# Spectral layers of a vision tower: inverse along h for two pairs at once in four banks, turning steps in one pair of banks

## The reference

```python
def spectral_conv(x, w1, w2):
    x_ft = jnp.fft.rfft2(x)
    out_ft = out_ft.at[:, :, :M1, :M2].set(jnp.einsum('bixy,ioxy->boxy', x_ft[:, :, :M1, :M2], w1))
    out_ft = out_ft.at[:, :, -M1:, :M2].set(jnp.einsum('bixy,ioxy->boxy', x_ft[:, :, -M1:, :M2], w2))
    return jnp.fft.irfft2(out_ft, s=(h, w))
...
for i in range(LAYERS):
    x1 = spectral_conv(h, w1, w2)
    x2 = jnp.einsum('bchw,oc->bohw', h, conv_w[i]) + conv_b[i][None, :, None, None]
    h = layer_norm(x1 + x2, ln_g[i], ln_b[i])
    if i < LAYERS - 1:
        h = gelu(h)
```

## Time and profile before

| | us |
|---|---|
| median of 3 runs | 5721.86 |
| lowest, highest | 5716.95, 5734.56 |
| profiled execution, its own time | 5729.41 |
| its span | 5727.7 |
| PE busy | 5285.1 (92%) |
| DVE busy | 4230.7 (74%) |
| ACT busy | 3896.4 (68%) |
| POOL busy | 630.8 (11%) |

### The profile page before, as it was taken

How to read it: one execution, slowest core, us unless ns; L and a number is a source line. 1 busy time by engine, 2 the same in 40 slices (tenths; PEclk the granted TensorE clock), 3 DMA queues, 4 the chain that set the end, 5 groups by cost and what they waited for, 6 DMA issues and landing times.

```text
span 5727.7 us, 135011 instructions
## 1 busy us (share of the span) xinstructions
PE 5285.1 (92%) x43556; PEld 2997.1 (52%) x43556; DVE 4230.7 (74%) x7712; ACT 3896.4 (68%) x6261; POOL 630.8 (11%) x943
## 2 busy tenths in 40 slices
PE   5887789999999999999999999999999999868778
PEld 2444456666666666666666654433333333334443
DVE  5888899999998999999999975555555555454553
ACT  5898776788666788666888656677777777523333
POOL 0133100233000233000233000000000000000000
PEclk9999999999999999999999999999999999877888
DMA  1334467667676667677676762221111111000000
GB/s 65 124 137 148 137 189 215 217 215 230 200 228 206 217 215 230 201 228 221 211 228 224 210 183 70 75 60 51 46 52 52 52 52 52 13 4 4 7 7 4
DMA packets 397185, 756.31 MB, mean 132 GB/s; under 512 B 245041, under 2 KB 303410, under 8 KB 331322
## 3 DMA queue, kind: packets, MB, share of 16 engines
q1 hardware_dynamic: 377402, 704.04, 38.8%
q0 software_dynamic: 19456, 48.01, 3.7%
HBM read 397.49 MB, written 354.42 MB: 131 GB/s over the span
## 4 chain that ended last, share of the span: by engine, by line
PE 81%; DVE 9%; issue 5%; ACT 3%; SPq 1%; DVEq 0%; ACTq 0%; DMA 0%
PE ps_y L914 18%; PE ps_y L907 9%; PE ps_t L926 9%; PE ps_t L1016 8%; PE ps_t L935 8%; PE ps_f L948 4%; PE ps_f L1001 3%; PE ps_s L893 3%; PE ps_f L986 3%; PE ps_s L961 3%; PE ps_t L1025 2%; PE ps_t L346 2%; PE ps_y L883 2%; ACT big L1169 1%; PE ps_f L336 1%
## 5 line engine op out<-in xcount | busy, mean ns | idle before, releaser
L1146 ACT ACTIVATE big<-ps_y 128x512 f32<-128x512 f32 x1280 | 777.0, 607 | 762.2 <-PE ps_y L914 699.6
L914 PEld LDWEIGHTS ps_y<-conv_now,big 128*128 128x128 f32 x8192 | 993.2, 191 | 520.2 <-issue 520.2
L1309 DVE TENSOR_REDUCE big<-big 128x16 f32<-128x512 f32 x1280 | 841.8, 679 | 522.5 <-ACT big L1146 522.3
L914 PE MATMUL ps_y<-conv_now,big 128*128 128x128 f32 x8192 | 1147.2, 283 | 0.0
L1302 DVE TENSOR_TENSOR big<-big 128x512 f32<-128x512 f32 x1280 | 932.1, 748 | 69.3 <-PE ps_t L926 62.2
L1155 ACT ACTIVATE big<-ps_t 128x512 f32<-128x512 f32 x1024 | 622.4, 608 | 334.2 <-PE ps_t L935 328.5
L926 PE MATMUL ps_t<-ident,big 128*128 128x128 f32 x5120 | 790.5, 277 | 43.9 <-DVE big L1302 42.5
L1162 ACT ACTIVATE big<-ps_t,g_now 128x512 f32<-128x512 f32 x1024 | 809.0, 790 | 9.3 <-PE ps_t L926 8.0
L1150 ACT ACTIVATE big<-ps_y 128x512 f32<-128x512 f32 x1280 | 780.1, 609 | 0.0
L926 PEld LDWEIGHTS ps_t<-ident,big 128*128 128x128 f32 x5120 | 587.6, 142 | 260.9 <-issue 204.8
L935 PE MATMUL ps_t<-ident,big 128*128 128x128 f32 x4096 | 654.4, 283 | 55.9 <-ACT big L1155 55.9
(11 more groups left out here) (180 smaller groups left out, 6419.0 us busy)
## 6 DMA issues: line engine op xcount, KB each, us to landing
hstore<-big SPq DMA_DIRECT2D x256, 1024.0 KB, 4.0
big<-hstore SPq DMA_DIRECT2D x256, 1024.0 KB, 5.3
xmodes<-x_out SPq DMA_DIRECT2D x128, 312.0 KB, 4.4
y_kt<-ymodes SPq DMA_DIRECT2D x512, 78.0 KB
ymodes<-y_st SPq DMA_DIRECT2D x192, 144.0 KB, 3.0
mix_room<-xmodes SPq DMA_DIRECT2D x48, 336.0 KB, 7.1
mix_room<-xmodes SPq DMA_DIRECT2D x48, 288.0 KB, 6.2
ymodes<-y_st SPq DMA_DIRECT2D x64, 192.0 KB, 3.4
```

What stands on the lines that cost most here:

```text
L914: last = mm(ps_y[:, wh, 128 * b:128 * b + 128], h_in[k // 2][:, at:at + 128], conv_now[:, :], start=False, stop=(b == 3))
L1146: af(y_sq[wh], ps_y[:, wh, :], ACT.Square).then_inc(s["sq_done"], 1)
L1309: v_.tensor_reduce(ss[:, k // 2, at:at + 16], groups(y_sq[wh]), AX.X, ALU.add).then_inc(s["ss_done"], 1)
```

## The change

Where the front is a layer and the back is not yet the head (`both` in the code), `inv_h` runs in slots 0 and 2 only and does both pairs of its half quad: eight matmuls in eight tiles, the even pair into ps_y and the odd pair into ps_f. `conv`, `square` and `keep_y` of an odd slot use ps_f (`y_of`). The steps with a turn (`inv_w`, `fwd_h`, `fwd_w`) all use ps_s, each with a wait for DVE's turn of the step ahead of it. `fwd_w` moves from the end of slot 1 to the middle of it, behind the first conv. `mix` of these quads goes to ps_y and stands ahead of the first conv of slots 1 and 3. On DVE, `turn_modes` moves from slot 2 to slot 1, behind `normed` and the products' sums, and `mix` behind `normed`. In the head `inv_h` stays with one pair at a time.

In all stages the turns write adjacent elements. To undo that, the matmuls of `inv_h` and `fwd_w` read runs of 16 or 13 adjacent elements and write their result to PSUM with 32 elements between neighbours.

```diff
-            def inv_h(n, k):
+            def inv_h(n, k, both):
...
+                for odd in odds:
+                    for image in range(2):
+                        for wh in range(2):
+                            r, half = slice(64 * image + 32 * wh, 64 * image + 32 * wh + 32), image ^ odd
+                            mm(y_of(odd, both)[64 * half:64 * half + 64, wh, :].rearrange("p (w o) -> p o w", o=32), c_inh[r, :],
+                               z_kx[j][r, :].rearrange("p (o w) -> p o w", w=32)[:, :, 16 * odd:16 * odd + 16],
+                               start=True, stop=False)
...
-                            last = mm(ps_s[at:at + 32, sx, 0:RUN], c_fww[r, :], t_w[r, j, 512 * sx:512 * sx + RUN],
+                            last = mm(ps_s[at:at + 32, sx, 0:RUN].rearrange("p (k c) -> p c k", c=32), c_fww[r, :],
+                                      t_w[r, j, :].rearrange("p (c k) -> p c k", k=32)[:, :, 16 * sx:16 * sx + KX],
...
-                        fwd_h(n - 1, 0, mixed)
+                        fwd_h(n - 1, 0, ps_s if both else ps_f, 0 if both else mixed, 0, n - 1 if both else 0, 0)
...
-                        inv_h(n, k)
-                        conv(k, 0)
+                            wait(pe, "tw_done", 2 * n - 3)
+                        if k % 2 == 0:
+                            wait(pe, "mix_read", mixed)
+                            inv_h(n, k, True)
+                        elif visit is not None:
+                            mix(*visit, ps_y, 2 * (4 * n + k))
+                        conv(k, 0, True)
+                        if k == 1 and back2 in STORED:
+                            fwd_w(n - 2, 2 * i + 2, 0)
...
-                v_.transpose(z_kx[j].rearrange("p (w o) -> p o w", o=32), flat(of).rearrange("p (k o) -> p o k", o=32)
+                v_.transpose(z_kx[j].rearrange("p (o w) -> p o w", w=32), flat(of).rearrange("p (k o) -> p o k", o=32)
...
-                    if k == 2 and back2 in STORED:
+                    if k == 2 and back2 in STORED and not both:
                         turn_modes(n - 2)
...
+                    if visit is not None and both:
+                        mix(*visit, ps_y)
+                    if k == 1 and back2 in STORED and both:
+                        turn_modes(n - 2)
```

More of the change, by code:

```diff
@@ L323, in attention_pool, with y_of @@
             nc.gpsimd.memset(ones, 1.0).then_inc(a["ones"], 1)
+        def y_of(odd, both):
+            return ps_f if both and odd else ps_y
         s_flat, f_flat = (t[:, :, :].rearrange("p a n -> p (a n)") for t in (ps_s, ps_f))
@@ L890, in inv_w @@
                 wait(pe, "fw_read", fw_count)
+                wait(pe, "tw_done", tw_count)
                 for sx in range(2):
@@ L903, in inv_h, with conv @@
                 wait(pe, "y_read", 2 * (4 * n + k))
-                for image in range(2):
-                    for wh in range(2):
-                        r, half = slice(64 * image + 32 * wh, 64 * image + 32 * wh + 32), image ^ odd
-                        mm(ps_y[64 * half:64 * half + 64, wh, :], c_inh[r, :], z_kx[j][r, 512 * odd:512 * odd + 512],
-                           start=True, stop=False)
-            def conv(k, wh):
+                for odd in odds:
[5 more added lines that the diff above has]
+                               start=True, stop=False)
+            def conv(k, wh, both):
                 for b in range(4):
                     at = 512 * (2 * (k % 2) + wh) + 128 * b
-                    last = mm(ps_y[:, wh, 128 * b:128 * b + 128], h_in[k // 2][:, at:at + 128], conv_now[:, :],
+                    last = mm(y_of(k % 2, both)[:, wh, 128 * b:128 * b + 128], h_in[k // 2][:, at:at + 128], conv_now[:, :],
                               start=False, stop=(b == 3))
@@ L942, in fwd_h @@
                 then(pe, "mix_read", mixed)
+                then(pe, "iw_read", iw_count)
+                then(pe, "fw_read", fw_count)
+                then(pe, "y_read", y_count)
                 for odd in range(2):
@@ L1036, in body @@
                         mixed = mixed + 2
+                    inner = back1 == "head"
+                    both = front in MIXED and not inner
                     if k == 0 and back2 in STORED:
-                        fwd_h(n - 2, 1, mixed)
+                        fwd_h(n - 2, 1, ps_s if both else ps_f, 0 if both else mixed, 2 * i + 1 if both else 0, 0,
+                              8 * n if inner else 0)
                     if k == 2 and back1 in STORED:
-                        fwd_h(n - 1, 0, mixed)
-                    inner = back1 == "head"
+                        fwd_h(n - 1, 0, ps_s if both else ps_f, 0 if both else mixed, 0, n - 1 if both else 0, 0)
                     pair = 4 * (n - 1 - LAST) + k
@@ L1050, in body @@
                         visit = (part, chunk, seq, ph, k - 1, count, tw_count)
-                    if visit is not None and not inner:
-                        mix(*visit, 0)
+                    if visit is not None and front == "stem":
+                        mix(*visit, ps_f, 0)
                     turned = 2 * (4 * n + k - 3)
@@ L1075, in body @@
                     if front in MIXED:
-                        conv(k, 1)
+                        conv(k, 1, True)
                     if k == 0 and front in MIXED:
-                        inv_w(n, 1, n - 2, ps_s)
-                    if k == 1 and back2 in STORED:
-                        fwd_w(n - 2, 2 * i + 2 if front in MIXED else 0, 0)
+                        inv_w(n, 1, 0, 2 * n - 2, ps_s)
+                    if k == 1 and back2 in STORED and front == "stem":
+                        fwd_w(n - 2, 0, 0)
                     if k == 2 and nxt in MIXED:
-                        inv_w(n + 1, 0, n - 1, ps_s)
+                        inv_w(n + 1, 0, n - 1, 2 * n - 1 if both else 0, ps_s)
             def head_slot(n, k, pair, turned, front, back2, kind, nxt, mixed, visit):
@@ L1331, in rsqrt_half, with mix @@
                 v_.scalar_tensor_tensor(r, t, 1.5, r, ALU.add, ALU.mult).then_inc(step, 1)
-            def mix(part, seq, k, count):
+            def mix(part, seq, k, count, of):
                 k0 = PARTS[part][0]
@@ L1371, in body @@
                     visit = (part, seq, k - 1, 2 if k == 1 else PARTS[part][1] - 2) if part is not None and k % 2 == 1 else None
-                    if visit is not None and not inner:
-                        mix(*visit)
+                    both = front in MIXED and not inner
+                    if visit is not None and front == "stem":
+                        mix(*visit, ps_f)
                     if inner:
@@ L1377, in body @@
                     if k == 0 and back2 in STORED:
-                        turn_w(n - 2, 1)
-                    if k == 2 and back2 in STORED:
+                        turn_w(n - 2, 1, ps_s if both else ps_f)
+                    if k == 2 and back2 in STORED and not both:
                         turn_modes(n - 2)
                     if k == 2 and back1 in STORED:
-                        turn_w(n - 1, 0)
+                        turn_w(n - 1, 0, ps_s if both else ps_f)
                     if k == 1 and front in MIXED:
```

60 lines of the change are left out of this document (30 added, 30 removed).

## The result

| | us |
|---|---|
| before, median on the same chip | 5724.9 |
| after, median of 4 runs (lowest, highest) | 5879.6 (5869.4, 5889.0) |
| ratio, 95% interval | 1.0263 (1.0245 to 1.0281) |
| forecast | 5794 (5630 to 5910) |

The change makes the kernel 155 us slower. The sign and the main wait were forecast, and the range held the time; the forecast loss was 72 us, less than half of what was measured.

What follows compares the result with a forecast made beforehand. PE was taken to bound layers and head. Product quads +91 us, quads without products -24, first stage -15 and clock +20 gave +72 us; against the median 5721.9 that is 5794 us, range 5630 to 5910.

Steps and rivals of the forecast that it cites:

- The sign: Whole kernel: the change makes it slower, chance 0.78, against 0.14 for faster and 0.08 for same.
- PE's own work: Layer quads: PE's work falls by 1.85 us without products and by 1.45 us with products.
- The new wait: fwd_h of slot 2 waits for DVE's turn_modes: 1.1 us without products, 3.3 us with, 200 us in all.
- Turns: DVE's turns, now writing adjacent elements, take 1.28 us instead of 1.99, 2.8 us per layer quad off DVE.
- First stage: Stage ahead of the layers: shorter turns take off 15 us over 32 quads, within 0 to 45.
- Rivals B: DVE's turns stay at 1.99 us, so DVE becomes the limit in the layers; 5870 us; chance 0.15.
- rival C: Matmuls with strided PSUM results, layers and head: streaming costs double, 422 us more, 6216 us; chance 0.12.
- Rival D: Layer quads: the stall is not there, PE's full saving of 160 us remains; 5547 us; chance 0.13.
- The clock term: Product quads: idle PE lowers the granted clock, costing 0.4 us each within 0 to 1.7, +20 us in all.
- Quads without products: Layer stage, 48 quads: -1.85 + 1.1 = -0.75 us, made -0.5 by px late in slot 3 by 0.3; -24 us.
- rival A's range: The forecast itself, 5690 to 5900 us by the ends of its terms; chance 0.60.
- The head: Stage after the layers: DVE has room there, so the shorter turns gain nothing.

Runs made afterwards that it cites:

- e3: The kernel before with only the layout changed: turns write adjacent elements, matmuls write strided results, still one pair at a time; 5697.8 us, ratio 0.9947.
- e2: The kernel after with turn_modes moved in DVE's queue between normed for wh 0 and normed for wh 1; 5693.1 us, ratio 0.9953.
- e10: The kernel with turn_modes between the two normed, plus turn_z moved ahead of the two sums of slots 0 and 2; 5670.0 us, ratio 0.9895.
- e11: The kernel with turn_modes and turn_z moved earlier, plus ACT's second scaling of w2 moved from slot 3 to the end of slot 2; 5661.0 us, ratio 0.9885.
- e5: The kernel after with 13 spare matmuls between conv of slot 1 and fwd_h of slot 2 in the 49 product quads; 5808.1 us, ratio 1.0136.

## Why the prediction was right or wrong

Right, by its own steps:

- PE's own work: 1.80 us less per quad without products against 1.85. The group of inverses along h takes 0.59 + 0.40 us in the chain and then the conv, for eight tiles what four took (1.02).
- The new wait: 204.4 us, 97 times, 3.15 and 1.04 us against 200 us, 3.3 and 1.1. It came from reading which turn_out the second normed waits for.
- Turns at 1.24 us (forecast 1.28). First stage 19 us shorter (forecast 15, picked between 0 and 45, so its nearness is in part luck). Rivals B and C are out: e3 alone shows both the short turn and the free strided result. The rule of the Trainium skill behind rival C (Advanced Engine Details and Errata, PSUM Cachelines: non-contiguous patterns slow matmuls significantly) does not show for these f32 matmuls, 526 ns against 523 with 128 bytes between neighbours; the measurement decides.
- Rival D had the right cure (without the stall the kernel is faster), but not its worth: e2 is that case, and gives 5693 where D had 5547. Most of the 160 us of PE work went into small waits: in the layers PE waits some 170 us in e2 against some 45 in the kernel before, and stands 44 us at half clock against 14. e10 and e11 gave 32 us back.

Wrong, in two terms:

- **The clock term.** I gave 0.4 us per product quad within bounds of 0 to 1.7, because one row of mixed stretches was all there was, and took a value near the low end. Filling the stall gave 71 us, 1.46 per quad, near the high end; forecast 20. This term was mis-sized by 51 us. A row with idle time spread over many gaps said little of one gap of 3 us. Without the clock the product quad takes 29.24 us; the forecast had 29.5.
- **Quads without products.** The step that failed is the one from -0.75 to -0.5 us, in which px late by 0.3 is all that is added to the stall: I looked for lateness only at the two new places and took DVE to be in time everywhere else. fwd_w moved forward on PE while turn_z, which frees its banks, kept its place behind two sums on DVE: 0.72 us. px came to 0.92 instead of 0.48, and turn_w was late by 0.17. I forecast -24 us and got 48 x 0.57 = +27 by the quad shown; by the mean of all 48 (25.72 against 25.30) it is +20. The gap of 0.48 in the earlier trace rows, which the prediction took for a wait on px_done, stands there as "issue" and is left in e11 when px is in time.

The sum at the start of the head, in us: product quads without the clock 49 x 1.60 = +78, clock +71 to +80 (the second from the start of the head in e5, 3480.3), quads without products +27, first stage -19: +157 to +166, against 161 measured. By the means of all quads the split is a little different (product quads without the clock 29.5 against 27.8, +83; the others +20), and the sum the same within 2 us. In rival A's range the ends of the terms add up to 5714 and 5943 and not to 5690 and 5900; the measured time lies in both. The head, which I gave nothing, took nothing; the last 11 us between 161 there and 150 at the end lie behind it, in the attention and expert stage, which the change does not touch. From the last fc1 to the end the traces of these kernels take 748 to 764 us, with no order by the change (after 751, before 761), so these 11 us are not an effect of it.

## What to carry to other kernels

When a step is moved forward on the engine that sets the end, list every buffer that the step needs freed and move the work that frees it too; here moving three short operations (DVE's turn_modes and turn_z and a scaling of ACT's) turned 2.6% slower into 1.1% faster. A stall of 3 us on PE cost 1.46 us more than its length here, because matmuls behind it ran at half the clock: price it from a row of a comparable single gap, or measure it by filling the gap with spare matmuls. And where one change joins two that can be had apart, time them apart: the layout alone gained 30 us, so by difference the rest lost 185.

## What the runs showed of the hardware

- Half clock behind one idle gap: behind 3.15 us fwd_h took 1.09 to 1.96 us and the turning behind it up to 1.04 and 0.85 instead of 0.59 and 0.44; behind 2.10 us fwd_h mostly kept 1.09 and the groups behind it were slow, with 113 us at half clock in the layer stage against 188; behind 1.04 us there were 10. 3.17 us of spare matmuls in the gap brought the stage back to 21 us, 14 in the kernel before.
- A small DVE operation can be held for as long as a POOL operation runs: 0.20 us became 11.81 under a fill of 16.75 us, 0.23 became 1.91 under an addition of 1.85 us. Not all are held: turns from PSUM ran beside POOL unchanged, and under the fill so did a TENSOR_TENSOR of DVE (0.69 us), which POOL's addition does hold (2.89 us for the two of L1322). The Trainium skill (SBUF — State Buffer, SBUF: two separate sides) tells of ports that DVE and GpSimd share under an exclusive lock for a whole instruction, taken by DVE for operations with two SBUF inputs against a GpSimd one that reads SBUF, and for its two-port modes. The rows of L1351 and L1322 agree; that TENSOR_SCALAR, with one input, is held by a fill would fit its two-port mode, which no run here tests.
- For DVE's turns the written side set the price: 1986 ns with a strided read and write, 1245 with the same strided read and an adjacent write. For ACT's copy a strided read with a write in runs of 4 was as dear (1304 ns) as an adjacent read with a strided write (1317).
- A PSUM result with 128 bytes between neighbours costs an f32 matmul nothing (526 ns against 523), and eight tiles of 32 x 64 pass in the time of four.
